# x's integers in the gate stage of a gated FFN block: transposed by DMA in place of TensorE

## The reference

```python
def act_qdq(x):
    qmax = 2.0 ** (ACT_BITS - 1) - 1.0           # 16 bits
    scale = jnp.maximum(jnp.max(jnp.abs(x)) / qmax, 1e-12)
    return jnp.clip(jnp.round(x / scale), -qmax - 1.0, qmax) * scale
...
x = act_qdq(x)                                     # x: the normed tokens, 4096 x 512
up = act_qdq(x @ lpbq_dequant(w_up).T)             # w: 1536 x 512, 4 bits in blocks of 32
gate = act_qdq(x @ lpbq_dequant(w_gate).T)
sig = fixed_qdq_u16(jax.nn.sigmoid(gate))
gate = act_qdq(gate * sig)
o = act_qdq(gate * up)
return o @ lpbq_dequant(w_down).T
```

## Time and profile before

| | |
|---|---|
| median of 3 runs | 1497.55 us (1496.6 to 1497.62) |
| the profiled execution | 1497.72 us, its span 1496.0 us |
| PE busy | 1330.1 us, 89% of the span |
| DVE, ACT, POOL busy | 1016.6, 644.9, 268.3 us |
| the gate stages | from 571.1 us to about 864 us of the span |

### The profile page before, as it was taken

How to read it: one execution, slowest core, us unless ns; L and a number is a source line. 1 busy time by engine, 2 the same in 40 slices (tenths; PEclk the granted TensorE clock), 3 DMA queues, 4 the chain that set the end, 5 groups by cost and what they waited for, 6 DMA issues and landing times. The chain is left out here.

```text
span 1496.0 us, 18874 instructions
## 1 busy us (share of the span) xinstructions
PE 1330.1 (89%) x6142; PEld 1087.1 (73%) x6142; DVE 1016.6 (68%) x1397; ACT 644.9 (43%) x769; POOL 268.3 (18%) x312
## 2 busy tenths in 40 slices
PE   7899999999999967999999989999993019999999
PEld 6677767768777846788888868888882018888887
DVE  0477667767766643777777769999998984545453
ACT  3334333333333313434333245556667973333331
POOL 1123214313422310000000135551120000000000
PEclk9999999999999988999999999999996559999999
DMA  8012212311311119776664789996558963444443
GB/s 309 1 41 96 90 37 84 98 52 61 126 49 48 44 49 365 253 241 244 247 245 154 265 301 324 317 317 204 176 193 333 324 230 106 168 157 159 173 145 117
DMA packets 111248, 259.77 MB, mean 174 GB/s; under 512 B 10832, under 2 KB 23120, under 8 KB 109648
## 3 DMA queue, kind: packets, MB, share of 16 engines
q1 hardware_dynamic: 110896, 259.04, 49.6%
q10 hardware_dynamic: 288, 0.00, 0.0%
HBM read 152.04 MB, written 106.95 MB: 173 GB/s over the span
## 5 line engine op out<-in xcount | busy, mean ns | idle before, releaser
L1070 PE MATMUL gpG<-xph,Wh 128*128 128x512 f32 x384 | 152.5, 397 | 3.0 <-DVE xpl L990 2.0
L1544 PE MATMUL pD<-Wh,xph 128*128 128x512 f32 x384 | 150.7, 393 | 4.6 <-DVE xpl L1523 4.6
L1070 PE MATMUL pU<-xph,Wh 128*128 128x512 f32 x384 | 150.4, 392 | 1.0 <-POOLq L63 1.0
L1544 PE MATMUL pD<-Wl,xph 128*128 128x512 f32 x384 | 150.6, 392 | 0.0
L1070 PE MATMUL gpG<-xph,Wl 128*128 128x512 f32 x384 | 150.5, 392 | 0.0
L1544 PE MATMUL pD<-Wh,xpl 128*128 128x512 f32 x384 | 150.4, 392 | 0.0
L1070 PE MATMUL gpG<-xpl,Wh 128*128 128x512 f32 x384 | 150.1, 391 | 0.0
L1070 PE MATMUL pU<-xpl,Wh 128*128 128x512 f32 x384 | 149.9, 390 | 0.0
L1070 PE MATMUL pU<-xph,Wl 128*128 128x512 f32 x384 | 149.9, 390 | 0.0
L1523 DVE TENSOR_TENSOR xpl<-doq,xph 128x1536 fp32r<-128x1536 int16 (+1 forms) x34 | 56.4, 1664 | 124.1 <-ACT xph L1490 124.1
L973 ACT ACTIVATE gst<-gpG,sc 128x512 f32<-128x512 f32 x96 | 66.4, 692 | 171.0 <-PE gpG L1070 163.2
(11 more groups left out here) (172 smaller groups left out, 2935.4 us busy)
## 6 DMA issues: line engine op xcount, KB each, us to landing
dub<-up_d SPq DMA_DIRECT2D x42, 768.0 KB, 4.7
gate_d<-gst SPq DMA_DIRECT2D x96, 256.0 KB, 2.3
gb<-gate_d SPq DMA_DIRECT2D x32, 768.0 KB, 6.3
up_d<-ust SPq DMA_DIRECT2D x96, 256.0 KB, 4.1
xr<-xn_d SPq DMA_DIRECT2D x9, 1024.0 KB, 6.1
xph<-up_d SPq DMA_DIRECT2D x11, 768.0 KB, 6.3
xpl<-up_d SPq DMA_DIRECT2D x11, 768.0 KB, 6.4
xin<-in_x SPq DMA_DIRECT2D x32, 256.0 KB, 2.7
```

The source lines that it names most:

```text
L1070: mm = pe.matmul(ps[:, :], Ws[:, it, kt * P:(kt + 1) * P], xs[:, kt, :], start=(kt == 0 and Ws is Wh and xs is xh), stop=(kt == KT - 1 and ...
L1544: mm = pe.matmul(pD[4 * t + q][:, :], os_[n][:, cs], Ws[:, it, :], start=(it == 0 and os_ is oh and Ws is Wh), stop=(it == IT - 1 and os_ ...
```

## The change

For the stages T = 1 to 7, ACT makes the integers from x's rows as they lie (`integers`: four activations of 128x512, float32 in SBUF to int16 in the new tile `xi`, behind it = 2), and SP turns them with four DMA transposes of 128x512 int16 (128 KB each, SBUF to SBUF, one for each 128 tokens) into `xq`, behind the store of it = 4. `high` moves to it = 7 to 10 and waits for all four transposes, `low` to it = 8 to 11. The load of `xr` behind it = 6 waits for the integers in place of the transposes. PE's 16 transposes are left for stage 0 alone.

```diff
--- before.py
+++ after.py
@@ -852,6 +852,7 @@
         Wh, Wl = W
         xh, xl = ([pair[part] for pair in x_pair] for part in range(2))
         xr = [sb(ph, f"xr{n}", [P, 4, H], F32) for n in range(2)]
+        xi = sb(ph, "gxi", [P, 4, H], I16)
         xq = [sb(ph, f"gxq{n}", [P, KT, 512], I16) for n in range(2)]
         gmx = sb(ph, "gmx", [P, 2, FT * IT], F32)
         NS = 4
@@ -866,6 +867,7 @@
         st_out = [sem(f"g_st_out{n}", 16) for n in range(NS)]
         xT_ps, xq_done, xh_done, g_ps, g_neg = (sem(f"g_{n}") for n in ("xT_ps", "xq", "xh", "ps", "neg"))
         xl_done = sem("g_xl", KT)
+        xi_done, apart, xt_in = sem("g_xi"), sem("g_apart"), sem("g_xt_in", 16)
         g_sb, g_pos = sem("g_sb", 4), sem("g_pos", NS)
         red = sem("g_red")
         block = ph.enter_context(nc.Block())
@@ -906,10 +908,20 @@
                         for n in range(NJ):
                             sp.wait_ge(*at(J.stored[n], 0, 32 * (2 * c + 1)))
                         load_w[1](sp, c)
+                    if it == 4 and not (last and t):
+
+                        if t:
+                            sp.wait_ge(*at(xl_done, 2 * KT * i, KT))
+                        else:
+                            sp.wait_ge(*at(xl_done, 2 * KT * i, 0))
+                        for q in range(4):
+                            sp.wait_ge(*at(xi_done, 8 * i, 4 * t + q + 1))
+                            sp.sem_inc(apart, 1)
+                            sp.dma_start_transpose(xq[(t + 1) % 2][:, :, q * P:(q + 1) * P], xi[:, q, :]).then_inc(xt_in, 16)
                     if it == 6 and not last:
 
                         src = rows((2 * i + (t + 3)) % FT)
-                        sp.wait_ge(*at(xT_ps, 2 * KT * i, KT * t + 2 * KT))
+                        sp.wait_ge(*at(xi_done, 8 * i, 4 * t + 4))
                         sp.dma_start(xr[(t + 1) % 2][:, :, :], src).then_inc(xr_in[(t + 1) % 2], 16)
                     if it in (2, 6, 10) and not (last and 3 * t + it // 4 + 2 >= JR):
                         q = 3 * t + it // 4
@@ -945,21 +957,24 @@
 
         @block.scalar
         def _(act):
-            def parts(i, T):
-
-                n = T % 2
-                for kt in range(KT):
-                    act.wait_ge(*at(xT_ps, 2 * KT * i, KT * T + kt + 1))
-                    if T:
-                        act.wait_ge(*at(xl_done, 2 * KT * i, KT * (T - 2) + kt + 1))
-                    act.activation(xq[n][:, kt, :], pX[kt][:, :], ACT.Copy, scale=INV_X).then_inc(xq_done, 1)
+            def integers(i, T):
+
+                act.wait_ge(*at(xr_in[T % 2], 16 * i, 16 * (T // 2 + 1)))
+                act.wait_ge(*at(xt_in, 128 * i, 64 * (T - 1)))
+                for q in range(4):
+                    act.activation(xi[:, q, :], xr[T % 2][:, q, :], ACT.Copy, scale=INV_X).then_inc(xi_done, 1)
 
             def high(i, T, kt):
-                act.wait_ge(*at(xq_done, 2 * KT * i, KT * T + kt + 1))
+                if isinstance(i, int) and i == 0 and T == 0:
+                    act.wait_ge(xq_done, kt + 1)
+                else:
+                    act.wait_ge(*at(xt_in, 128 * i, 64 * T))
                 act.wait_ge(*at(x_out[T % 2], 32 * i, 32 * (T // 2)))
                 act.activation(xh[T % 2][:, kt, :], xq[T % 2][:, kt, :], ACT.Copy).then_inc(xh_done, 1)
 
-            parts(0, 0)
+            for kt in range(KT):
+                act.wait_ge(xT_ps, kt + 1)
+                act.activation(xq[0][:, kt, :], pX[kt][:, :], ACT.Copy, scale=INV_X).then_inc(xq_done, 1)
             for kt in range(KT):
                 high(0, 0, kt)
             def evictions(i, last=False):
@@ -971,10 +986,10 @@
                         act.wait_ge(*at(st_out[n], 32 * IT // NS * i, 16 * (m // NS)))
                         act.wait_ge(*at(g_pos, 2 * IT * i, m - NS + 1))
                         act.activation(stage[n][:, :], pG[m % 3][:, :], ACT.Copy, scale=S_X).then_inc(g_sb, 1)
-                        if it == 4 and not (last and t):
-                            parts(i, t + 1)
-                        if it in range(5, 5 + KT) and not (last and t):
-                            high(i, t + 1, it - 5)
+                        if it == 2 and not (last and t):
+                            integers(i, t + 1)
+                        if it in range(7, 7 + KT) and not (last and t):
+                            high(i, t + 1, it - 7)
                         if it in (3, 7, 11):
                             job_hi(act, J, i, 3 * t + it // 4)
 
@@ -998,8 +1013,8 @@
                         dve.wait_ge(*at(g_sb, 2 * IT * i, m + 1))
                         dve.tensor_reduce(gmx[:, 1, bass.ds(2 * IT * i + m, 1)], stage[m % NS][:, :], X, ALU.min).then_inc(g_neg, 1)
                         dve.tensor_reduce(gmx[:, 0, bass.ds(2 * IT * i + m, 1)], stage[m % NS][:, :], X, ALU.max).then_inc(g_pos, 1)
-                        if it in range(6, 6 + KT) and not (last and t):
-                            low(i, t + 1, it - 6)
+                        if it in range(8, 8 + KT) and not (last and t):
+                            low(i, t + 1, it - 8)
                         q = 3 * t + it // 4
                         if it % 4 == 0:
                             job_scale(dve, J, i, q)
@@ -1026,15 +1041,12 @@
 
         @block.tensor
         def _(pe):
-            def transposes(i, T):
-
-                n = T % 2
-                pe.wait_ge(*at(xr_in[n], 16 * i, 16 * (T // 2 + 1)))
+            def transposes():
+
+                pe.wait_ge(xr_in[0], 16)
                 for kt in range(KT):
-                    if T:
-                        pe.wait_ge(*at(xq_done, 2 * KT * i, KT * (T - 1) + kt + 1))
                     for q in range(4):
-                        mm = pe.transpose(pX[kt][:, q * P:(q + 1) * P], xr[n][:, q, kt * P:(kt + 1) * P], ident[:, :])
+                        mm = pe.transpose(pX[kt][:, q * P:(q + 1) * P], xr[0][:, q, kt * P:(kt + 1) * P], ident[:, :])
                     mm.then_inc(xT_ps, 1)
 
             def gates(i, last=False):
@@ -1049,12 +1061,10 @@
                         else:
                             ready = None
                         product(pe, pG[m % 3], Wh, Wl, xh[t], xl[t], it, ready).then_inc(g_ps, 1)
-                        if it == 3 and not (last and t):
-                            transposes(i, t + 1)
                         if it % 4 == 3:
                             job_turn(pe, J, i, 3 * t + it // 4, ident)
 
-            transposes(0, 0)
+            transposes()
             with pe.Fori(0, FT // 2 - 1) as i:
                 gates(i)
             gates(FT // 2 - 1, last=True)
```

## The result

Over 20 runs each, the changed kernel takes **1495.4 us** (median; 1492.2 to 1500.62), the kernel before 1499.86 us (1496.6 to 1503.66). The ratio is 0.997, with a 95% interval of 0.9962 to 0.9979: 4.5 us less (3.1 to 5.7). A second set of the same kernel gave 0.9956 (0.9941 to 0.9972), 6.6 us less. The forecast was a gain of 7.5 us, to 1490.1 us. The first interval ends short of it; the second reaches it. The forecast set out from 1497.55 us, the median of the first 3 runs, and 20 runs of the same kernel have 1499.86, so gains are to be compared and not end times. One of the 6 runs of `again_after` (2340.93 us) and one of the 8 of `before_again` (1661.7 us) were slow ones, at a lower granted clock, and their medians and ratios leave them out.

What follows compares the result with a forecast made beforehand. PE's instruction stream was taken to bound the gate stages. Removed transposes 10.5 us plus stage 0's 0.5, less 3.5 of new waits, gave 7.5 us: 1497.55 to 1490.1 us, range 1485.3 to 1502.

Steps and rivals of the forecast that it cites:

- the price of the transposes: PE, gate stages: each group of 16 transposes costs 1.75 us by distance of starts; six later stages give 10.5 us.
- the wait at a stage's start: PE at kt = 3 of a stage's first product waits for `low(3)`: 0.5 us at 7 steps, 3.5 us lost.
- shift as a block: Everything behind the gate stages was taken to move earlier unchanged, since the up stage starts from PE's last gate product.
- Stage 0 gains 0.5 us in place of 1.75: Stage 0: PE waits longer for product 4's eviction, so removing transposes gains zero there; 0.5 us comes from moved `parts` activations.
- The transfers: Four transposing DMAs a stage land within a 9.4 us budget, 2.35 us each in series, at no cost.
- Rivals A and B: Transposing transfers late at ACT's `high(0)`: A costs the whole gain or more, chance 0.20; B 1 to 10 us, 0.14.
- the one microsecond that the prediction named as a sign of being wrong: ACT waiting for the transposing DMA ahead of `xph` by more than about a microsecond would show the forecast wrong.
- the estimate in series: By the skill's 1309 ns a square, 16 squares a stage take 20.9 us, with the end near 1571 us.
- Rival C: `low(3)` is in time, PE does not wait at the stage's start, 3.5 us stay: 1486.5 us; chance 0.10.
- SP can lose some 7 us here without harm: SP's queue behind the four transfers: product 5's store, job's load and `xr` are needed late enough to allow 7 us delay.
- the third sign of being wrong: The landing of `gate_d` growing so that evictions wait for it would show the forecast wrong.
- Rival D: Stage 0: PE's clock falls to 1.2 GHz after the idle, costing about 3 us: 1493; counted within the forecast's 0.56.

Runs made afterwards that it cites:

- again_after: The changed kernel run once more, nothing altered, to see the spread of its parts: 1494.71 us, ratio 0.9956 to the kernel before.
- before_again: The kernel before run once more, unchanged, to see its front phase and what such a set bears: 1500.52 us, ratio 0.9999.
- low10: Changed kernel with `low(3)` behind it = 10, next to `low(2)`, in place of it = 11: 1487.29 us, ratio 0.9913 to the kernel before.
- pe_t1: Changed kernel with PE also doing the 16 transposes of T = 1 in stage 0, result unread: 1493.03 us, ratio 0.9961 to the kernel before.
- before_ns6: The kernel before with six tiles `gst` in place of four: 1495.75 us, ratio 0.998 to the kernel before.
- late_before: The kernel before, all transposes on PE, with only `high` and `low` moved to the change's places: 1502.07 us, ratio 1.0016.
- six: Changed kernel with two of the four transposing transfers issued twice, six a stage: 1501.9 us, ratio 1.0018 to the kernel before.
- six_xr8: Changed kernel with six transfers a stage and the 1 MB `xr` load moved from it = 6 to it = 8: 1496.01 us, ratio 0.9976 to before.
- low10_again: Changed kernel with `low(3)` behind it = 10, repeated later on another chip: 1490.14 us, ratio 0.9941 to the kernel before.
- double: Changed kernel with each transposing transfer issued twice, eight a stage, the extras unread: 1520.05 us, ratio 1.0144 to the kernel before.
- before: The kernel before the change, nothing altered, as the reference of the ratios: 1499.86 us over 20 runs.
- low10_ns6: Changed kernel with `low(3)` behind it = 10 and six tiles `gst` in place of four: 1487.34 us, ratio 0.9927 to the kernel before.

## Why the prediction was right and where it was wrong

The direction, the price of the transposes and the place of the new wait were right, and the gain was smaller than forecast: 4.5 us (3.1 to 5.7) in the time of the whole program in place of 7.5. Two steps failed. In the gate stages the term for the wait at a stage's start was too small, 3.5 us where 4.6 were measured, so that the stages gave 6.54 us. And the sum puts the rest of the program at nothing: it lets what follows shift as a block and names nothing ahead of the stages or outside the span, and 2 of the stages' 6.54 us are missing there.

- **The price of the transposes, 1.75 us by the distance of starts**: right. `low10` has 35.82 - 34.07 = 1.75 us in each stage.
- **Stage 0 gains 0.5 us in place of 1.75**: right, 0.63 in the one profile and 0.32 in the other. `pe_t1` shows the other side, and `before_ns6` (37.17 us) that the wait for product 0's store is what makes this stage long. PE's idle ahead of product 7 was to be 2.7 us and is 2.59.
- **The transfers**: in time from T = 1 on, as forecast, by the row of the `gate_d` store: 2.3 us there, 2.4 measured. Rivals A and B fall with it. In stage 0, for which no budget was worked out, they were late: ACT waits 2.1 us for them, 3.6 in the second profile, above the one microsecond that the prediction named as a sign of being wrong. In the first profile this cost nothing inside stage 0 (11.41 us from `job_turn` behind it = 7 to that behind it = 11, 11.40 before), in the second 0.45 us. SP's part was taken too low: the nearest row had 0.33 us an issue, measured are 1.19, 5.3 us for the four. The Trainium skill ("VectorE: DVE Perf Modes", the three transpose paths) gives 1309 ns for one 128x128 square of bf16 by DMA, and the estimate in series was 20.9 us for 16. The trace does not agree with that reading in series: a transfer of 128x512 int16, four squares, takes SP 1.19 us and lands in 2.4, and 16 squares are in after 6.5 us, 0.41 us each.
- **The wait at a stage's start: 0.5 us**: this is the term of the sum that was mis-sized. It measures 0.59 to 0.61 us in T = 2 to 6 (0.58 to 0.62 in `late_before`), 0.45 in T = 7, and 1.13 in T = 1: 4.6 us in place of 3.5. In the second profile T = 1 has 1.45, and the sum is 5.0. Rival C, no such wait, is excluded by the change and made real by `low10`, at 1487.3 us beside the 1486.5 reckoned.
- **"SP can lose some 7 us here without harm"**: this step failed, and it is where T = 1's second half microsecond comes from. The prediction asked when each transfer behind the four is needed and counted product 5's store, the job's load and `xr`. Product 7's store was left out. It stands behind the 1 MB load. Already in the kernel before it landed in 5.3 us, with 5.2 us of slack and not 7; with the change it lands in 6.8 and has 1.8. In stage 0 of the changed kernel itself there is none: the store is issued at 608.55 and lands 6.7 us later, at 615.25, and the eviction of product 11 starts at 615.34, where 2.72 us behind the one before would be 614.77. The 0.57 us pass through the extremes and `low(3)` to PE, which idles 0.84 us there in place of 0.31. The profile puts this idle of ACT down to PE; in the second profile, where the store is issued at 610.29 and lands at 617.1, it names nothing. ACT's timeline, changed kernel and then the second profile:

```profile
612.05 0.69 ACT L988 ACTIVATE gst<-gpG,sc 128x512 f32<-128x512 f32 x1 [1.51 <-PE gpG L1080]
...
615.34 0.69 ACT L988 ACTIVATE gst<-gpG,sc 128x512 f32<-128x512 f32 x1 [2.08 <-PE gpG L1080]
```

```profile
617.17 0.69 ACT L988 ACTIVATE gst<-gpG,sc 128x512 f32<-128x512 f32 x1 [2.83 <-issue]
```

`six` makes it a cost of about 1 us in every other stage, and `six_xr8` takes that away by moving the load alone. The landing of `gate_d` growing until an eviction waits for it was the third sign of being wrong that the prediction named. For T = 1 of the changed kernel itself the cause is read from these times; no run moved the load in it alone.
- **Rival D, the clock**: it came true in the changed kernel (8 matmuls 0.2 us later each, 1.6 us where 3 were priced), and cost nothing that the profile shows, because DVE's chain ended last behind it anyway.
- **ACT**: the integers from SBUF take 710 ns each where a third of a longer row gave 520. ACT has room, and nothing follows from it.

**What stays open.** The stages gain 5.8 to 6.5 us, the whole program 4.5 (3.1 to 5.7) in 20 runs. Of the difference 0.3 us lie outside the profiled span: in the set of `again_after` the device time is 2.06 us above the span for the changed kernel and 1.77 for the kernel before. Up to 0.6 us may be the first load, below. From the last `job_turn` of the stages to the end of the span the two profiles of the kernel before take 635.0 and 635.6 us, those of the changed kernel 635.8 and 634.9, which shows no difference. The rest, about 1 us, is not explained; the front phase's pause (`before_again`) may be in it, since nothing shows how many of the 20 runs of either kernel have it. It is small beside what sets of few runs vary by: the gain of the whole program is 2.4 us above that of the stages in `low10` and 2.2 below it in `low10_again`, the same kernel. `double`'s 3.1 us and more a stage was not split further between x's lateness, the store and the job.

## What to carry to other kernels

When instructions are inserted in a queue, list every transfer behind them with the time by which its tile is needed again, and take its landing from where it stands in the queue: here a store behind a 1 MB load took 5.3 us before the change and 6.8 after it, where the median of all stores had been 2.3. Slack has to be counted for the stage as it will be: the shorter stage alone took 1.2 us of this one. Work taken off the bounding engine paid in full only where its stand-in was ready before the engine got there: moving one 0.68 us DVE instruction by one product (`low10`) gave 4.1 to 5.2 us more in the stages, beside 5.8 to 6.5 by the change itself (in one set 0.9913 in all against 0.9956). And where the first stage has other limits than the rest, treat it separately: of the last 3.7 us in the stages (279.24 to 275.55) 0.8 came with 6 tiles `gst` and 2.9 with leaving PE its transposes there.

## What the runs showed of the hardware that was not expected

- A DMA transpose of 128x512 int16 from SBUF to SBUF held SP's queue for 1.19 us (a store of 256 KB: 0.33), and up to 3.69 us while the DMA engines were at a share of 1.00 (`low10_ns6`).
- With four such transfers a stage the median landing of the 256 KB store went from 2.3 to 3.4 us, and the DMA engines from 0.69 to 0.82. Whether the load or the stores' new places in the queue did it was not separated. The transfers move small packets: the changed kernel has 26064 packets under 512 B, the kernel before 10832, which is 544 for each of the 28 transfers.
- In all ten profiles of kernels with DMA transposes the program's very first load, of `cx`, lands 6.2 to 6.4 us after its issue, in the four without them 5.0 to 5.2, though no transpose runs within 570 us of it. PE's timeline, changed kernel and then the kernel before:

```profile
7.18 1.94 PE L815 MATMUL pS<-ident,cx 128*128 128x128 f32 x8 [7.18 <-DMA cx<-in_ctx]
10.19 2.05 PE L827 MATMUL pS<-cT,wk 128*128 128x256 f32 x4 [1.07 <-DMA wk<-in_L_xattn_w_k]
```

```profile
5.88 1.94 PE L815 MATMUL pS<-ident,cx 128*128 128x128 f32 x8 [5.88 <-DMA cx<-in_ctx]
9.58 2.90 PE L827 MATMUL pS<-cT,wk 128*128 128x256 f32 x6 [1.76 <-DMA wk<-in_L_xattn_w_k]
```

Of 1.3 us, 0.6 are left by L827. The cause was not tried.
- TensorE's granted clock fell to the 1.2 GHz level behind the idle ahead of product 7 in all seven profiles in which that idle was 2.47 to 2.83 us, and stayed at 2.4 GHz behind 0.73 to 0.98 us at the same place (`pe_t1`, `before`, `late_before`, `before_again`). In the kernel before it also stayed there behind an idle of 2.36 us ahead of `job_turn`.
